# A two-layer vision tower on one core: Mamba's inputs and its first scan steps in another order, token 0 of the scan apart, the gate tile by tile, the maxima of the last quantiser later, and down projections begun with five of eight tiles

## The reference

```python
h = tok_attention(x)                 # 16 heads of 16, 512 tokens, softmax
h = concat([cls_tok, h], axis=1)     # T = 513 tokens of 256
h = h + diag_scan_block(layernorm(h))
h = h + bit_ffn_conv(layernorm(h))   # quantised rows and weights, depthwise conv, silu
h = h + mamba(layernorm(h))
h = h + bit_ffn_gated(layernorm(h))  # silu(gate) * up, quantised, down projection

# mamba, per batch entry, DI = 512 channels, NS = 16 states
xv = silu(depthwise_conv4(x @ W_in[:512].T)); z = x @ W_in[512:].T
dt = softplus(x[:, :64] @ W_dt.T + b_dt);  B, C = x @ W_B.T, x @ W_C.T
for t in range(513):                 # h0 = 0
    h = exp(dt[t] * A) * h + (dt[t] * xv[t]) * B[t]
    y[t] = h @ C[t]
y = (y * silu(z)) @ W_out.T
```

## Time and profile before

| what | value |
|---|---|
| median of three executions | 2632.63 us (2632.61 to 2637.04) |
| profiled execution, its own time | 2640.73 us |
| its span | 2638.8 us |
| PE, DVE busy | 2095.6 us, 2085.3 us (79% each) |
| ACT, POOL busy | 1314.3 us, 1213.1 us |
| TensorE's granted clock over the span | 0.922 of 2.4 GHz |

### The profile page before, as it was taken

How to read it: one execution, slowest core, us unless ns; L and a number is a source line. 1 busy time by engine, 2 the same in 40 slices (tenths; PEclk the granted TensorE clock), 3 DMA queues, 4 the chain that set the end, 5 groups by cost and what they waited for, 6 DMA issues and landing times.

```text
span 2638.8 us, 24318 instructions
## 1 busy us (share of the span) xinstructions
PE 2095.6 (79%) x8500; PEld 1138.2 (43%) x8500; DVE 2085.3 (79%) x2433; ACT 1314.3 (50%) x1882; POOL 1213.1 (46%) x567
## 2 busy tenths in 40 slices
PE   2998887778699887778779898677877988867786
PEld 0326663235333766223542376422453256643244
DVE  5865869996785586999688467899878748789977
ACT  0563356564265435655417544565443744456543
POOL 1220248992222025999222111799722212289952
PEclk9999898999899988899989998898989999889998
DMA  5200000000220000000022000000003100000000
GB/s 180 89 13 0 1 0 0 0 0 1 69 85 1 0 1 0 0 0 0 1 85 70 1 1 0 0 0 0 0 1 116 37 1 1 1 0 0 0 1 16
DMA packets 41072, 51.26 MB, mean 19 GB/s; under 512 B 9072, under 2 KB 32368, under 8 KB 40944
## 3 DMA queue, kind: packets, MB, share of 16 engines
q1 hardware_dynamic: 40944, 49.62, 6.1%
HBM read 26.25 MB, written 10.49 MB: 14 GB/s over the span
## 4 chain that ended last, share of the span: by engine, by line
PE 47%; DVE 25%; POOL 13%; ACT 7%; issue 6%; DMA 1%; SPq 0%; POOLq 0%; DVEq 0%; ACTq 0%
PE psum L691 13%; PE psum L955 12%; POOL big L1904 9%; PE psum L818 5%; POOL big L1893 4%; ACT big L1075 3%; PE psum L806 3%; PE psum L791 3%; DVE mid L1679 3%; PE psum L754 2%; ACT mid L1075 2%; DVE mid L1397 2%; PE psum L972 2%; DVE mid L1325 2%; DVE negmax L1507 2%
## 5 line engine op out<-in xcount | busy, mean ns | idle before, releaser
L955 PE MATMUL psum<-big,ident 128*128 128x512 f32 x992 | 520.1, 673 | 181.9 <-POOL big L1904 181.2
L1758 DVE TENSOR_TENSOR_SCAN big<-psum,b,big 128x512 f32<-128x512 f32 x512 | 615.7, 1275 | 11.9 <-ACT psum L1075 11.9
L1075 ACT ACTIVATE big<-psum 128x1024 f32<-128x1024 f32 (+2 forms) x592 | 447.7, 776 | 259.4 <-PE psum L806 145.1
L1904 POOL TENSOR_TENSOR big<-big 128x2048 f32<-128x2048 f32 x124 | 560.1, 4517 | 27.8 <-DVE big L1758 27.8
L1075 ACT ACTIVATE psum<-mid,aneg 128x512 f32<-128x512 f32 x512 | 353.6, 692 | 256.7 <-DVE big L1758 256.7
L955 PEld LDWEIGHTS psum<-big,ident 128*128 128x128 f32 x992 | 202.8, 214 | 456.6 <-POOL big L1904 234.5
L1507 DVE TENSOR_REDUCE negmax<-psum 128x1 f32<-128x512 f32 x512 | 318.6, 678 | 48.3 <-PE psum L791 47.2
L1893 POOL TENSOR_TENSOR big<-mid,big 128x512 f32<-128x512 f32 (+1 forms) x128 | 222.8, 1740 | 25.9 <-ACT big L1075 25.9
L791 PE MATMUL psum<-mid 96*128 96x512 bf16 x512 | 189.5, 391 | 34.8 <-DMA mid<-mid 23.9
L806 PE MATMUL psum<-mid 98*128 98x512 bf16 x512 | 181.9, 382 | 20.0 <-ACT big L1075 14.0
L1696 DVE TENSOR_TENSOR big<-mid,psum 128x1536 f32<-128x1536 f32 (+1 forms) x128 | 188.7, 1475 | 5.9 <-PE psum L934 5.7
(11 more groups left out here) (206 smaller groups left out, 3528.9 us busy)
## 6 DMA issues: line engine op xcount, KB each, us to landing
mid<-mid SPq DMA_DIRECT2D x192, 64.0 KB, 2.6
mid<-scratch SPq DMA_DIRECT2D x192, 64.0 KB, 2.2
scratch<-big SPq DMA_DIRECT2D x4, 1536.0 KB, 6.1
out<-hres SPq DMA_DIRECT2D x8, 513.0 KB, 6.8
big<-in_x SPq DMA_DIRECT2D x8, 512.0 KB, 4.6
big<-in_w SPq DMA_DIRECT2D x2, 1024.0 KB, 6.3
big<-in_wg SPq DMA_DIRECT2D x1, 1024.0 KB, 9.8
big<-in_wu SPq DMA_DIRECT2D x1, 1024.0 KB, 11.7
```

What stands on the lines that cost most here:

```text
L955: mm = nc.tensor.matmul(y_psum[:, c], ident[:, :], st(1, k)[:, c], start=(n == 0), stop=(n == NS - 1))
L1075: return nc.scalar.activation(o, a, func, **kw)
L1758: V.tensor_tensor_scan(st(0, k)[:, c], a_psum(DT * k + c), st(0, k)[:, c], b0[:, p, n, c:c + 1], ALU.mult, ALU.add).then_inc(scanned, 1)
L1904: G.tensor_tensor(st(1, k), st(0, k), c_row(k).unsqueeze(1).broadcast_to([P, DT, S]), ALU.mult).then_inc(hc_ready, 1)
```

## The change

Seven edits, none of which adds a product or leaves one out:

1. down_project replaces both down projections: per p, five k-tiles of both products after q_first, then three after q_ready.
2. PE's order of Mamba's inputs was d(0) d(1) bc(0) bc(1) x(0) x(1) z; it becomes d(0) bc(0) bc(1) d(1) x(0) first x(1) z. `first` takes a slot of its own instead of a bank of the scan.
3. ACT's and DVE's lists follow: p = 0's softplus and its step sizes come before p = 1's; one rounding stands between the two splits of bc.
4. dt*x of token 0 is computed on its own by DVE (dx0), so b0 and the first output y0 no longer read POOL's array; spread waits for POOL's array of its own p only. project_first does both entries in one product of two columns, into the C row's bank.
5. In step 0 of the scan, spread(1) comes between the scans of tiles 1 and 2, and ACT's copies move to match.
6. The gate of the first entry is four instructions, each behind one scan of step 17, in place of one ahead of them; add_y(16) waits tile by tile.
7. T3 and I3, S3 of p = 0 stand four and two products later on PE, one loop step later on DVE and ACT; I2 and S2 of p = 1 are taken up one step later on ACT and DVE.

```diff
-BETWEEN = {4: (("T2", 1),), 8: (("I2", 1), ("S2", 1)), 16 + 8: (("T3", 0),), 16 + 12: (("I3", 0), ("S3", 0))}
+BETWEEN = {4: (("T2", 1),), 8: (("I2", 1), ("S2", 1)), 16 + 12: (("T3", 0),), 16 + 14: (("I3", 0), ("S3", 0))}
-AT_T2, AT_I2, AT_T3, AT_I3 = 2, 4, HT + 6, HT + 9
+AT_T2, AT_I2, AT_T3, AT_I3 = 2, 5, HT + 7, HT + 10
...
+                def down_project(f, name, wt):
+                    for p in range(PAIR):
+                        for c in range(KT):
+                            slot_free(f"{name}{c}", p)
+                        for tiles in (range(DVE_TILES), range(DVE_TILES, HT)):
+                            if tiles[0]:
+                                pe.wait_ge(q_ready, q_of(2 * f + 1, p))
+                            else:
+                                pe.wait_ge(q_first, PAIR * f + p + 1)
+                            for c in range(KT):
...
-                    pe.wait_ge(q_ready, q_of(1, p))
-                    for c in range(KT):
-                        fill(f"g{c}", p, [(w2[:, k, c * P:(c + 1) * P], mid_bf(p, 5, HT)[:, k]) for k in range(HT)])
+                down_project(0, "g", w2)
...
+                step_products(0)
+                for p in range(PAIR):
+                    if p:
+                        pe.wait_ge(ln_normed, q_of(3, p))
                     fill("bc", p, [(wbc[:, k], big_un(p)[:, k]) for k in range(KT)], rows=96)
+                step_products(1)
+                inputs("x", wx, 0)
+                slot_free("first", 0)
+                pe.wait_ge(bc_first, 1)
+                nc.tensor.matmul(flat_slot("first", 0)[:, 0:PAIR * 32], ones96[:, :], ...
+                inputs("x", wx, 1)
...
                 spread_b(0)
+                project_first()
+                spread_b(1)
                 spread_c(0)
...
+                split_bc(0)
+                round_up(0)
+                split_bc(1)
...
+                taps(0, 0)
+                taps(0, 1)
+                round_up(1)
+                taps(0, 2)
+                taps(0, 3)
+                step_sizes(0)
+                for c in range(DT):
+                    taps(1, c)
...
+                step_sizes(1)
+                dve.wait_ge(dt_ready, PAIR)
+                dve.wait_ge(m_silu, DT * PAIR)
...
+                V.tensor_tensor(dx0[:, :, :], both[:, :, 2, :, 0], both[:, :, 0, :, 0], ALU.mult).then_inc(
...
+                dve.wait_ge(z_silu, DT * PAIR)
+                for p in range(PAIR):
+                    V.scalar_tensor_tensor(out=y0[:, :, p], in0=dx0[:, p], scalar=s0[:, p:p + 1],
...
                         V.tensor_tensor_scan(st(0, k)[:, c], a_psum(DT * k + c), st(0, k)[:, c], b0[:, p, n, c:c + 1],
                                              ALU.mult, ALU.add).then_inc(scanned, 1)
+                        if k == 0 and c == 1:
+                            spread(1)
+                        if k == NS + 1:
+                            gate(c)
```

More of the change, by code:

```diff
@@ L140, in plan_fills @@
     ln(3)
-    each(*[f"d{c}" for c in range(DT)])
+    order.extend((f"d{c}", 0) for c in range(DT))
     each("bc")
-    each(*[f"x{c}" for c in range(DT)])
+    order.extend((f"d{c}", 1) for c in range(DT))
+    order.extend((f"x{c}", 0) for c in range(DT))
+    order.append(("first", 0))
+    order.extend((f"x{c}", 1) for c in range(DT))
     each(*[f"z{c}" for c in range(DT)])
@@ L1204, in _, with step_inputs @@
                 layer_norm(3)
-                for p in range(PAIR):
+                def step_inputs(p):
                     for c in range(DT):
@@ L1216, in first_tap, with silu, silu_z @@
                                   scale=col("mw", 4 * c + 3)).then_inc(m_tap0, 1)
[L1218 to L1225 removed]
+                def silu(p, c):
+                    act.wait_ge(m_tap, 3 * (DT * p + c) + 3)
+                    run(mid4(p, 0)[:, c], mid4(p, 0)[:, c], ACT.Silu).then_inc(m_silu, 1)
+                def silu_z(p, c):
+                    wait_full(act, f"z{c}", p)
+                    run(mid4(p, 1)[:, c], slot(f"z{c}", p), ACT.Silu).then_inc(z_silu, 1)
+                step_inputs(0)
+                absolute(0)
+                exponential(0)
+                step_inputs(1)
+                logarithm(0)
+                first_tap(0, 0)
+                absolute(1)
+                first_tap(0, 1)
+                first_tap(0, 2)
+                exponential(1)
+                first_tap(0, 3)
+                wait_full(act, "first", 0)
+                run(first[:, :, :].rearrange("p b r -> p (b r)"), flat_slot("first", 0)[:, 0:PAIR * 32],
+                    ACT.Copy).then_inc(first_copied, 1)
+                logarithm(1)
                 nc.scalar.preload_act_table(ACT.Silu)
@@ L1256, in _ @@
                         k = NS * p + n
-                        if k == 1:
-                            act.wait_ge(w_first_full, 1)
-                            run(wy0[:, :], y_psum[:, 0, 0:PAIR * KT], ACT.Copy).then_inc(w_first, 1)
                         for c in range(DT):
@@ L1270, in _ @@
                             if c == 1:
+                                if k == 0:
+                                    copy_b(0)
+                                    act.wait_ge(w_first_full, 1)
+                                    run(wy0[:, :], c_psum[:, 0:PAIR * KT], ACT.Copy).then_inc(w_first, 1)
                                 if k >= 2:
@@ L1649, in _, with split_bc @@
                 layer_norm(3, lambda p: hres[:, p])
-                for p in range(PAIR):
+                def split_bc(p):
                     ps, dst = slot("bc", p, 96), bcp[:, p, 0:T]
```

172 lines of the change are left out of this document (79 added, 93 removed).

## The result

The changed kernel takes 2608.36 us (median of 4 runs, 2607.8 to 2610.8), the kernel before on the same chip 2634.84 (4 runs, 2632.6 to 2639.0): a ratio of 0.989, interval 0.987 to 0.991. The gain is 26.5 us; forecast were 45.6, and 2587 us with a range that ended at 2607. So the direction was right, and the time lies 1.4 us outside the range. The forecast started from a median of 2632.63 us; as a ratio to that, the range ended at 0.990, and the measured 0.989 lies just inside it.

A forecast was written before the change was run, and what follows sets the result against it. No engine bounds it all, PE and DVE being busy nearly equally, so stages were taken singly. 1.7 + 0.8 + 2.0 + 1.4 + 5.5 = 11.4 us a turn, 45.6 in four, gave 2587 us, range 2560 to 2607.

The forecast's parts named there:

- Scan start: From layer norm 3 to the scan: step 1's scans start at 1053.0 instead of 1054.88, taken as 2.0 us a turn.
- The rival of no collision: In the second split DVE and POOL do not collide: 6.5 instead of 2.0 us a turn, 2569 us; chance 0.2.
- the collision: In the second split, POOL's operations of 4.5 us each hold DVE's SBUF instructions; first taps at 1010.0 to 1011.3, not 1008.52.
- Down projection of g: First feed-forward block: products begin after five rounded tiles, DVE's wait of 0.99 goes, adds move up by 1.7 us.
- Down projection of y: Second feed-forward block: products begin after the first rounded tiles, gaining 0.8 us a turn.
- the wait for y1 is only 0.78: Second block's down projection: DVE waits just 0.78 us for y1, so the gain there is 0.8 us.
- Gate: Step 17 of the scan: quarter gates between the scans end them 0.6 + 2.1 instead of 4.1 late, gaining 1.4 us.
- the fourth is behind the last scan: Gate at step 17: four instructions cost some 0.1 us each more than one, but the fourth follows the last scan.
- Second block: Second feed-forward block: with T3 four products later, DVE's waits for PE shrink, gaining 5.5 us a turn; bounds 1.5 and 8.2.
- 9.2 - 1.0 - 1.3 - 1.4: Second block: DVE's waits, less those ahead of the moved places, a new U6 wait, and maxima held by POOL: 5.5 us.
- the waits only move: Second block: waits only move to U6 and T3, 1.5 instead of 5.5 us a turn, 2603 us; chance 0.17.

The follow-up runs named there:

- The first experiment: Against the changed kernel, DVE does both splits and bc first and only then the rounding of p = 0 that lets POOL begin: 2594.3 us.

## Why the prediction was right and where it was wrong

- **Scan start (2.0 forecast, 2.7 measured): right in mechanism and size.** bc 5.5 after the first d product, first tap at 21.2, taps' stretch 21.4 and z's end at 51.5 were forecast as 5.5, 20 to 21.3, 21.5 and 52. From there to step 1's scans 10.6 us were measured (2.96 to the first scan, 6.10 to the end of step 0's scans, 1.56 more); I had put 11.2, behind a z end 0.3 later. The rival of no collision (0.2) is out. The first experiment shows what the collision costs as it stands: 6.3 us at the first tap, 2.55 at the end. What the list of collisions left out is b0, held for 4.58 us; that this cost nothing is luck, as it lay beside the wait for z.
- **Down projection of g (1.7 forecast, 1.6): right.** A wait of 0.74 for g is left, as the products run at the lower clock, before and after (5.33 and 5.20 us for 32); fillers take it away.
- **Down projection of y (0.8; 0 in turns 2 and 3, 0.6 in the mean): the step that failed is "the wait for y1 is only 0.78", counted in full as 0.8.** It took for granted that p = 1's products keep the clock that they had (3.69 us for 32 in three turns of the kernel before), while the earlier p = 0 lets PE stand longer: they took 5.27, and the wait stayed at 0.81. With fillers it goes in three turns of four.
- **Gate (1.4, 1.0): right in mechanism.** POOL's wait is 1.46 (forecast 1.6), and its product of step 17 comes 1.6 us earlier. But two steps on only 1.1 of that are left and at the scan's end 1.0, since DVE's scans of step 18 come only 1.0 earlier: the fourth quarter gate of 0.67 stands ahead of the next spread. The step that was off is the one that put it at nothing, "the fourth is behind the last scan".
- **Second block (5.5, 2.5): the step that failed is "9.2 - 1.0 - 1.3 - 1.4".** Of DVE's 9.2 us of waits for PE, 4.9 lay behind T3 and went, up to the new 1.8 at U6 and 0.3 at T3. The other 4.2 lay in the first half; I let 1.0 of them stand, but no edit moves what they wait for: 3.3 are left, and 1.2 have been added at ACT. I had read ACT's 4.02 at I2 as a matter of its place in ACT's list, where it is PE's list and the slots that hold it. That put 3.2 us a turn, 13 in all, too much into the sum, and with the clock's two forms at I2's rows and 0.5 us of POOL on DVE's scaling it accounts for the block in the main. The rival "the waits only move" is nearer in size, with 1.5 for the block and 2603 us for the whole; yet its mechanism came true only in part, at I3 (2.58) and U6 (1.76).

The sum: 8.0 a turn by the profiles where 11.4 was forecast. Of the 3.4 missing the block has 3.0, the attention part 0.5, the gate 0.4, the projections 0.3; the scan start is 0.7 over. By the medians the gain is another 5.5 us less than by the profiles. So the total hides a term that missed upwards, the scan start, beside four that missed downwards.

## What to carry to other kernels

Before counting a wait as gone, ask at which instruction of the *other* engine's list it ends: a consumer moved later gains nothing if the producer's place, and the buffer it needs, stay as they were. When an engine's work comes to lie beside that of another which excludes it, as POOL did DVE here, list every instruction in that stretch that will be held, the small ones too, and put those first that have to be through: one line moved gave 2.6 us a turn here. And when work is taken from TensorE's way so that it stands idle longer, look at the clock of the next products; 16 fillers in that idle time brought it back, for 6 us in all.

## What the runs showed of the hardware

- DVE instructions with small SBUF operands were held for whole POOL operations: a CAST of 32 x 513 took 3.53 us instead of 0.42, a product of 64 columns 4.45 instead of 0.21, and, in the first experiment, a TENSOR_SCALAR of 2052 columns with one input 4.52 instead of 1.22. The last is not a case of two inputs. Products with one input in PSUM and reductions never were: in the changed kernel the taps take 0.74 to 0.75 us in 72 places beside POOL as elsewhere, and reductions of 512 columns 0.67 to 0.69. The Trainium skill ("SBUF — State Buffer", Who interferes with whom) says that casts and tensor_scalar may take the shared ports as well, and that the second to come blocks until the first is through; these rows agree.
- The same stretch of the same kernel, with the same wait of 2.5 us ahead of it, ran in some turns at TensorE's upper clock and in others at the lower, which is worth 1.5 us in the second block's first half and 1.2 up to its last rounding. The idle time alone does not tell which it will be: 32 products ran at the lower clock behind 2.38 us of it and at the upper behind 3.10. Medians of the kernel before lay from 2634.8 to 2639.9 us between the groups of runs; that the clock is the reason is not shown, but the stretches of the trace told more than the medians where 2 to 4 us were in question.
